# Mamba scans of 1024 columns in one instruction, and 12 instead of 13 of 32 products by C on GpSimd

## What is computed

```python
xz = jnp.einsum('bld,ed->ble', hidden_states, in_proj_w)
x, z = (xz[..., :d_inner], xz[..., d_inner:])
x_conv = sum((x_pad[:, w:w + L, :] * conv_w[:, w] for w in range(d_conv))) + conv_b
x_conv = _silu(x_conv)
x_dbl = jnp.einsum('bld,ed->ble', x_conv, x_proj_w)
delta = jax.nn.softplus(jnp.einsum('blr,dr->bld', dt_in, dt_proj_w) + dt_proj_b)
A = -jnp.exp(A_log)

def step(h, inp):
    d_t, B_t, C_t, u_t = inp
    dA = jnp.exp(d_t[:, :, None] * A)
    h = h * dA + (d_t * u_t)[:, :, None] * B_t[:, None, :]
    y = jnp.einsum('bdn,bn->bd', h, C_t)
    return (h, y)
```

## Time and profile before

| what | us |
|---|---|
| median of 3 runs | 6550.24 (6548.16 to 6550.28) |
| the profiled execution | 6549.9 |
| its span | 6548.2 |
| PE busy in the span | 6175.3 |
| DVE busy | 4267.1 |
| ACT busy | 3519.6 |
| POOL busy | 5132.0 |

### The profile page before, as it was taken

The page is one execution under the profiler, slowest core; times in us unless marked ns, Lnnn a source line. Parts: engine busy times, 40 slices in busy tenths (PEclk is TensorE's granted clock), DMA queues, the critical chain, the costliest instruction groups (busy, mean ns, idle before and its releaser), DMA issues. The chain is left out here.

```text
span 6548.2 us, 78761 instructions
## 1 busy us (share of the span) xinstructions
PE 6175.3 (94%) x25444; PEld 3970.3 (61%) x25444; DVE 4267.1 (65%) x5490; ACT 3519.6 (54%) x6418; POOL 5132.0 (78%) x3926
## 2 busy tenths in 40 slices
PE   7999999999999999999998799978999999999999
PEld 3444444444444444444443588866788888888888
DVE  6999999999999999999999377779100000000000
ACT  5677677767676777676766588750222222222222
POOL 6999999999999999999999677736454545454544
PEclk9999999999999999999999999989999999999999
DMA  3555555555555555555555244330566656566554
GB/s 124 166 162 171 166 168 166 168 165 168 165 172 163 166 165 166 170 164 169 166 163 167 62 121 122 116 120 1 175 190 179 190 179 189 180 189 179 183 162 135
DMA packets 551754, 1029.76 MB, mean 157 GB/s; under 512 B 77426, under 2 KB 245876, under 8 KB 516784
## 3 DMA queue, kind: packets, MB, share of 16 engines
q1 hardware_dynamic: 441168, 669.34, 33.3%
q0 software_dynamic: 110176, 355.39, 18.0%
HBM read 926.04 MB, written 88.72 MB: 155 GB/s over the span
## 5 line engine op out<-in xcount | busy, mean ns | idle before, releaser
L361 POOL TENSOR_TENSOR m_dbu<-m_du,m_bb 128x1024 f32<-128x1024 f32 x1024 | 2390.8, 2363 | 0.0
L739 PE MATMUL m_y_bank<-m_prod,m_ident 128*128 128x512 f32 x4096 | 1977.8, 612 | 143.1 <-POOL m_prod L370 143.1
L512 ACT ACTIVATE m_decay<-m_delta,m_a_neg 128x512 f32<-128x512 f32 x2048 | 1419.4, 695 | 724.7 <-DVE m_h L622 722.7
L739 PEld LDWEIGHTS m_y_bank<-m_prod,m_ident 128*128 128x128 f32 x4096 | 789.2, 196 | 1122.9 <-issue 907.2
L1734 DVE TENSOR_SCALAR e_ye<-e_ybank,e_listing 128x256 f32<-128x256 f32 x270 | 118.2, 479 | 1817.1 <-PE e_ybank L1768 1817.1
L622 DVE TENSOR_TENSOR_SCAN m_h<-m_decay,m_h_end,m_dbu 128x512 f32<-128x512 f32 x1024 | 1259.4, 1267 | 3.4 <-ACT m_decay L512 2.5
L622 DVE TENSOR_TENSOR_SCAN m_h<-m_decay,m_dbu 128x512 f32<-128x512 f32 x1024 | 1197.7, 1207 | 13.8 <-ACT m_decay L512 13.2
L1708 ACT ACTIVATE e_a<-e_ubank 128x512 f32<-128x512 f32 x540 | 322.5, 597 | 1473.6 <-PE e_ubank L1759 1473.6
L370 POOL TENSOR_TENSOR m_prod<-m_h,m_cb 128x1024 f32<-128x1024 f32 x416 | 982.5, 2362 | 20.0 <-issue 15.0
L1759 PE MATMUL e_ubank<-e_xT,e_w 128*128 128x256 f32 x4320 | 978.6, 380 | 1.3 <-ACT e_xT L1699 1.3
L1768 PE MATMUL e_ybank<-e_w,e_a 128*128 128x256 f32 x4320 | 954.5, 379 | 0.7 <-ACT e_a L1708 0.7
(11 more groups left out here) (216 smaller groups left out, 6663.9 us busy)
## 6 DMA issues: line engine op xcount, KB each, us to landing
m_bb<-rows_bc SPq DMA_DIRECT2D x1024, 256.0 KB, 3.8
m_cv<-rows_bc SPq DMA_DIRECT2D x608, 256.0 KB, 4.0
m_cb<-rows_bc SPq DMA_DIRECT2D x416, 256.0 KB, 3.4
m_xin<-in_x SPq DMA_DIRECT2D x32, 512.0 KB, 5.7
m_xres<-in_x SPq DMA_DIRECT2D x32, 512.0 KB, 5.6
x<-m_xres SPq DMA_DIRECT2D x32, 512.0 KB, 6.3
a_xa<-x SPq DMA_DIRECT2D x64, 256.0 KB, 2.9
a_xr<-x SPq DMA_DIRECT2D x64, 256.0 KB, 3.2
```

The source lines that it names most:

```text
L361: nc.gpsimd.tensor_tensor(dbu[:, slot], du[:, q[1], p * PC:(p + 1) * PC], bb[:, slot].unsqueeze(1).to_broadcast([P, PC, T]), ALU.mult).the ...
L512: nc.scalar.activation(decay[:, cc], delta[:, r, c], ACT.Exp, scale=a_neg[:, c, n:n + 1]).then_inc(decay_done, 1)
L739: ins = nc.tensor.matmul(y_bank[:, cc], ident[:], prod[:, slot, cc], start=False, stop=(n == NS - 1))
```

## The change

Each unit now gets one scan of 1024 columns, both groups one behind the other, in place of two of 512. So that the second group doesn't go on from the first, the decay of its first column is kept at zero (written once, and ScalarE writes only the other 511 columns). In second halves the start of the second group is added to its first column of `dbu` by a small ScalarE operation, `carry`: dbu + h_end * (first decay). The first decays of a block are computed ahead, 128x16 for each pass. Since a scan takes both groups' decays at once, there are two decay buffers, of even and odd units; the even one is the old one in PSUM, the odd one lies in SBUF. `sp_r` shrinks from four slots to two. Unit 13's product by C goes from GpSimd to VectorE. The waits for scans count units now; the decays wait for the scan of unit u-2, and the scan for both decays.

```diff
-    POOL_UNITS = [u for u in range(UNITS) if u % 5 in (1, 3)]
+    POOL_UNITS = [u for u in range(UNITS) if u % 5 in (1, 3) and u not in (13,)]
...
-        sp_r = sb("sp_r", [P, CH, T])
+        sp_r = sb("sp_r", [P, 2, T])
...
+        first_decay = sb("first_decay", [P, PASSES, NS])
+        decay_odd = sb("decay_odd", [P, PC, T])
         xres = sb("xres", [P, TB, H])
-        decay = al.ps("decay", [P, PC, T])
+        decay_even = al.ps("decay", [P, PC, T])
...
+        def decay_of(u):
+            return decay_odd if u % 2 else decay_even
...
+            for of in (decay_even, decay_odd):
+                nc.scalar.mul(of[:, 1, 0:1], ident[:, 0:1], 0.0).then_inc(s_a, 1)
...
                 elif kind == "dt":
-                    if i == 0:
-                        wait(act, delta_done, count(q, CH, 0))
-                    nc.scalar.activation(sp_r[:, i], bank, ACT.Relu, bias=vecs[:, 1, i:i + 1])
+                    wait(act, delta_done, count(q, CH, i - 1))
+                    nc.scalar.activation(sp_r[:, i % 2], bank, ACT.Relu, bias=vecs[:, 1, i:i + 1])
...
+            def carry(q, u):
+
+                start = dbu[:, u % RING, 1, 0:1]
+                wait(act, first_done, PASSES * (q[0] + 1))
+                wait(act, end_saved, carries(q[0], u))
+                wait(act, dbu_done, units_done(q, u))
+                nc.scalar.activation(start, h_end[:, u, 1:2], ACT.Identity, scale=first_decay[:, u // NS, u % NS:u % NS + 1],
+                                     bias=start).then_inc(carried, 1)
...
+                if r:
+                    wait(act, carried, carries(q[0] - 1, UNITS - 1))
+                    for p in range(PASSES):
+                        c = p * PC + 1
+                        nc.scalar.activation(first_decay[:, p], a_neg[:, c], ACT.Exp,
+                                             scale=delta[:, r, c, 0:1]).then_inc(first_done, 1)
...
                         if cc and earlier in VECTOR_UNITS:
                             copy_c(q, vector_upto(earlier) % VU)
-                        wait(act, scan_done, scans_done(q, u - 1, cc))
-                        nc.scalar.activation(decay[:, cc], delta[:, r, c], ACT.Exp,
+                        wait(act, scan_done, units_done(q, u - 2))
+                        nc.scalar.activation(decay_of(u)[:, cc, cc:], delta[:, r, c, cc:], ACT.Exp,
                                              scale=a_neg[:, c, n:n + 1]).then_inc(decay_done, 1)
+                        if cc and r:
+                            carry(q, u)
...
-                    n, slot = u % NS, u % RING
+                    slot = u % RING
+                    wait(dve, decay_done, decays_done(q, u))
+                    if r:
+                        wait(dve, carried, carries(q[0], u))
+                    wait(dve, dbu_done, units_done(q, u))
...
+                    nc.vector.tensor_tensor_scan(
+                        h[:, slot].rearrange("p c t -> p (c t)"), decay_of(u)[:].rearrange("p c t -> p (c t)"),
+                        dbu[:, slot].rearrange("p c t -> p (c t)"), h_end[:, u, 0:1] if r else 0.0,
+                        ALU.mult, ALU.add).then_inc(scan_done, 1)
+                    to, earlier = unit_at(q, u - 1)
+                    if earlier in VECTOR_UNITS and not (first(q) and u == 0):
+                        weigh_state(to, earlier)
                     for cc in range(PC):
-                        wait(dve, decay_done, scans_done(q, u, cc))
...
-                        nc.vector.tensor_tensor_scan(h[:, slot, cc], decay[:, cc], dbu[:, slot, cc],
-                                                     h_end[:, u, cc:cc + 1] if r else 0.0,
-                                                     ALU.mult, ALU.add).then_inc(scan_done, 1)
-                        if cc == 0:
-                            to, earlier = unit_at(q, u - 1)
-                            if earlier in VECTOR_UNITS and not (first(q) and u == 0):
-                                weigh_state(to, earlier)
                         finishing(q, PC * u + cc, not first(q))
                         if not last:
                             preparation(q, PC * u + cc, norm)
```

More of the change, by code:

```diff
@@ L202, in mamba_stage @@
         decay_done = sem("decay_done")
+        first_done = sem("first_done")
+        carried = sem("carried")
         scan_done = sem("scan_done")
@@ L235, in units_done, with decays_done, carries @@
             return count(q, UNITS, u + 1)
-        def scans_done(q, u, cc=PC - 1):
-            return count(q, POSITIONS, PC * u + cc + 1)
+        def decays_done(q, u):
+            return count(q, POSITIONS, PC * (u + 1))
+        def decay_of(u):
+            return decay_odd if u % 2 else decay_even
+        def carries(b, u):
+            return b * UNITS + u + 1
         @block.sync
@@ L357, in make_dbu @@
                 wait(pool, b_loaded[slot], count(q, 16 * (UNITS // RING), 16 * (u // RING + 1)))
-                wait(pool, scan_done, scans_done(q, u - RING))
+                wait(pool, scan_done, units_done(q, u - RING))
                 if u % NS == 0:
@@ L367, in weigh_state @@
                 wait(pool, c_loaded[C_BUFFER[k]], count(q, 16 * loads_into(C_BUFFER, k), 16 * loads_into(C_BUFFER, k, k + 1)))
-                wait(pool, scan_done, scans_done(q, u))
+                wait(pool, scan_done, units_done(q, u))
                 wait(pool, summed, units_done(q, u - RING))
@@ L492, in save_end @@
             def save_end(q, u):
-                wait(act, scan_done, scans_done(q, u))
+                wait(act, scan_done, units_done(q, u))
                 nc.scalar.copy(h_end[:, u], h[:, u % RING, :, T - 1]).then_inc(end_saved, 1)
+            def carry(q, u):
[5 more added lines that the diff above has]
+                                     bias=start).then_inc(carried, 1)
             def copy_c(q, k):
@@ L595, in preparation @@
                     wait(dve, soft_done, count(p, 2 * CH, 2 * c + 2))
-                    nc.vector.tensor_tensor(delta[:, p[1], c], side_bank[:, bank_of("dt", c)], sp_r[:, c],
+                    nc.vector.tensor_tensor(delta[:, p[1], c], side_bank[:, bank_of("dt", c)], sp_r[:, c % 2],
                                             ALU.add).then_inc(delta_done, 1)
@@ L600, in weigh_state @@
                 slot = u % RING
-                wait(dve, scan_done, scans_done(q, u))
+                wait(dve, scan_done, units_done(q, u))
                 wait(dve, c_copied, count(q, VU, vector_upto(u)))
@@ L609, in scan_block @@
                 for u in range(UNITS):
-                    n, slot = u % NS, u % RING
-                    for cc in range(PC):
-                        wait(dve, decay_done, scans_done(q, u, cc))
-                        if cc == 0:
[L614 to L621, removed]
-                        nc.vector.tensor_tensor_scan(h[:, slot, cc], decay[:, cc], dbu[:, slot, cc],
-                                                     h_end[:, u, cc:cc + 1] if r else 0.0,
-                                                     ALU.mult, ALU.add).then_inc(scan_done, 1)
-                        if cc == 0:
-                            to, earlier = unit_at(q, u - 1)
-                            if earlier in VECTOR_UNITS and not (first(q) and u == 0):
-                                weigh_state(to, earlier)
@@ new lines, in scan_block @@
+                    slot = u % RING
[3 more added lines that the diff above has]
+                    wait(dve, dbu_done, units_done(q, u))
+                    to, earlier = unit_at(q, u - RING)
+                    if not (first(q) and u < RING):
+                        wait(dve, prod_by_pool, count(to, PU, pool_upto(earlier)))
+                    if r:
+                        wait(dve, end_saved, q[0] * UNITS + min(UNITS, UNITS - RING + u + 1))
+                    else:
+                        wait(dve, end_saved, q[0] * UNITS + (u - RING + 1 if u >= RING else 0))
```

2 lines of the change are left out of this document (1 added, 1 removed).

## The result

| what | before | after |
|---|---|---|
| median of 4 runs, us | 6550.24 | 7774.19 |
| range | 6548.16 to 6550.28 | 7772.59 to 7780.17 |
| Mamba stage, us | 3541 | 4763 |
| one half (stage / 32), us | 110.7 | 148.8 |

The ratio is 1.187, with a 95% interval of 1.185 to 1.189: 1224 us slower. The forecast was 7820 us (7100 to 8000), slower with a chance of 0.94. All of the difference lies in the Mamba stage: from its end to the end of the span there are 2934 us, 2935 before.

What follows compares the result with a forecast made beforehand. GpSimd at its limit, with VectorE just under, bounds the state space stage. From 110.7 us a half, the copy's wait gives 130.4 (+630 us) and exclusion 150.4 (+1270 in all): 6549.9 + 1270 = 7820 us, range 7100 to 8000.

Steps and rivals of the forecast that it cites:

- Two engines near their limits, work hardly changed: State space stage, per half: VectorE's work goes from 107.4 to about 106 us, GpSimd's from 109.9 to 107.5.
- rival 4: Fused scans: a 1024-column scan differs from the slope by over 0.3 us, 300 us on or off the forecast; chance 0.03.
- The copy's wait: Scans wait for a decay behind ScalarE's copy of C, 1.31 us after each VectorE product, some 640 times.
- 130.4 us without exclusion: A half of the state space stage with the copy's wait alone, +630 us; bounds +390 and +870.
- the 3 us for ScalarE being late: Steps without a copy: ScalarE's decays, carry and preparation do not always fit in a scan; 3 us a half.
- Exclusion: Odd scans with two SBUF inputs and GpSimd's products lock each other out for an instruction; 150.4 us a half.
- floor of 144.8: GpSimd's time per half if odd scans and its products exclude each other: 107.5 + 0.8 idle + 16 x 2.28.
- the 1.1 us added for both engines being close: State space stage: VectorE's 149.3 us a half raised to 150.4 because GpSimd's 144.8 lies close.
- The sum: Whole kernel: 150.4 us a half against 110.7, +1270 us on 6549.9, giving 7820 us.
- Rival 1: State space stage: the copy's wait alone with no exclusion, 7180 us; chance 0.26.
- Rival 2: Odd scans and GpSimd's products share SBUF reads element by element: 7180 us if GpSimd pays, 7750 if VectorE; chance 0.15.
- Rival 3: The copy's wait is hidden and nothing excludes; GpSimd stays the bound at 108.3 us a half, 6475 us; chance 0.05.

Runs made afterwards that it cites:

- e5_both: The changed kernel with the copy of C behind the second decay and carry, and odd scans reading a constant PSUM column instead of decays: 6683.3 us, ratio 1.021.
- e6_one_input: As e5_both, but odd scans read their decays from SBUF and a constant PSUM column in place of the products by B: 6682.6 us.
- e4_odd_psum: The changed kernel with odd scans reading a constant PSUM column in place of SBUF decays, both groups' y sums in one bank: 7317.2 us.

## Why the prediction was right

- **Two engines near their limits, work hardly changed.** Right. The fused scans took 2282 and 2341 ns for 2.28 and 2.34, which also settles rival 4. Without both losses VectorE is busy for 3394 / 32 = 106.1 us a half (e5_both), for "about 106".
- **The copy's wait.** Right in its place, and near in number: 695 scans waited, 1.17 us on average, for about 640 times 1.3. The gap in second halves is 1.70 us for 1.43, of which 0.19 is the carry, 0.37 us and not the 0.185 of its nearest row.
- **130.4 us without exclusion.** 134.6 measured, inside its bounds. The term too small was the 3 us for ScalarE being late, together with the carry: even without the copy's wait, e5_both has 274 us before scans, 8.6 a half. The prediction counted ScalarE's own work there and took TensorE to have room. On average it has, but ScalarE waits for it between two decays, as the timeline above shows.
- **Exclusion.** That one engine holds the other out for most of an instruction carried over from attention. When it does so could not be read there: the operation in attention has one tensor input in SBUF, and e6_one_input shows that one is not enough for a scan. That the precedent fitted was in part luck. VectorE's loss per odd scan is 1.01 us for 1.18. What GpSimd loses when held out is 1.97 for 2.28, so its floor of 144.8 was too high: it is the 139.5 of the run in which it is the bound. And in the changed kernel it is held out only every second time: it is busy for 124 us a half and nowhere near a bound, so the 1.1 us added for both engines being close had no ground.
- **The sum.** 150.4 us a half forecast, 148.8 measured. Of the growth of 38.1 us, 16.1 are longer odd scans and 22.0 the rest, where 18.9 and 19.7 had been put, and 1.1 for the closeness. That the sum came out within 1.6 us is in part luck, since these errors partly cancel.
- **Rival 1** (7180, no exclusion) falls with the 1051 us of the odd decays alone. **Rival 2** (shared turns) falls with durations of either 2.36 or 4.3 us. **Rival 3** (faster, 6475) failed on more than its point of decision: even with exclusion and the copy's wait taken away, the time stays over the old one. The fusion saves 2.5 us of VectorE's work a half and puts more than that into waits, and the 108.3 left out the 3.2 us of waits that VectorE had before.

## What to carry to other kernels

Before two operations are fused, look at what the second of them was hiding: here it covered a copy and an exponential on another engine, 25 us of idle time a half in exchange for a saving of 2.5. A buffer that moves from PSUM to SBUF changes more than its place if it gives VectorE a second SBUF input beside a busy GpSimd; the cost was half a GpSimd instruction on average for VectorE, and most of the VectorE instruction for GpSimd whenever it had an instruction to start meanwhile. Where one operation needs two results of another engine, look at what stands between the two in that engine's list, and whom that waits for. And take an engine's need as its busy time and the waits that stay when its work changes: an engine at 97% was as much the bound as the one at 99%.

## What was not expected of the hardware

TensorE's granted clock in the Mamba stage, an average over times at its two levels of 1.2 and 2.4 GHz, fell from 0.97 to 0.90 when the engine was busy for 78% of it in place of 94%, and its matmuls into y took 667 ns on average for 612; in e4_odd_psum, with 134.6 us a half, the clock was 0.93. It cost nothing that these runs show: ScalarE waited for TensorE for 85 us of that stage, where it had waited 225 before, and VectorE's waits for y fell from 43 to 5 us. The ScalarE operation on one column with a scale and a bias from memory took 0.37 us, twice the copy of two columns.
